# A blocked attention kernel on one core: the scaling of the softmax probabilities moves from Pool to VectorE for three heads of four

## Chip, core and metric

The kernel runs on one core of one Trainium2 chip. The metric is the device time of one execution in microseconds (us), given as the median of several runs. In this text PE is TensorE, ACT is ScalarE, DVE is VectorE, Pool is GpSimd; PEld is TensorE's weight load.

## What is computed

For 8192 tokens of 512 numbers, all in float32, the output is the input plus two branches of its layer norm: a windowed attention and a feed-forward network with ternary weights. The change lies in the attention branch, which is, cut to what matters:

```python
# B = 1, S = 8192, H = 16 heads of Dh = 32, W = 128, nb = S // W = 64 blocks
qkv = (x @ Wqkv + bqkv).reshape(B, S, 3, H, Dh)
...
scores = jnp.einsum('bhnqd,bhnkd->bhnqk', qb, kwin) * scale      # each block sees itself and both neighbours: 128 x 384
mask = (jnp.abs(kpos - qpos) <= W) & (kpos >= 0) & (kpos < S)
scores = jnp.where(mask[None, None], scores, jnp.float32(-1e+30))
attn = jax.nn.softmax(scores, axis=-1)
out = jnp.einsum('bhnqk,bhnkd->bhnqd', attn, vwin)
out = out.reshape(B, H, S, Dh).transpose(0, 2, 1, 3).reshape(B, S, dm)
return out @ Wout + bout
```

## The kernel before

The program has two stages, one after the other. `feed_forward_stage` computes the layer norm, its transpose (written to DRAM in a high and a low part) and the feed-forward branch; it takes the first 1140 us or so. `attention_stage` does the rest and holds the change.

Attention goes over 128 steps t. A step takes one pair of token blocks, i = t // 4, and one group of four heads, c = t % 4. Its two token blocks are the halves b = 0 and b = 1 of the step, so that a step has eight blocks of probabilities of 128 x 384 numbers (128 x 256 at the two ends of the sequence), numbered u = 4 b + h. They lie in one tile, `probs`. For each of them:

- PE computes the scores (L1208), all four heads of a half together, in three passes of high and low parts;
- DVE subtracts the mask and takes the maximum (`find_max`, L1060), from PSUM to `probs`;
- ACT takes the exponential in place and its row sum (`exp`, L989);
- DVE inverts the four sums of a half in one instruction (`invert_sums`, L1067, into `sum_rcp`);
- Pool multiplies each head's probabilities by its inverted sum, in place (`normalise`, L949);
- PE transposes the result, block by block of 128 columns (`turn_probs`, L1222, into `pT_ps`, which has two places);
- ACT copies it to `pT` (`copy_pT`, L999);
- PE multiplies it by the values (`probs_times_values`, L1246), once a step for both halves.

Every engine has one queue, written out by hand and worked off in order. PE's queue for step t is: scores of half 0; then four quarters, each made of the transposes of one head of half 1 of step t-1 (`turn_probs(t - 1, 1, part)`) and six matmuls of a projection of queries and keys for step t+2 (job A, L1139, 128 x 256); scores of half 1; values times probabilities of step t-1; four quarters of transposes of one head of half 0 of step t and three matmuls of a job B (values, L1148, or the output projection, L1157, 128 x 512). Half of the steps have the one kind of job B, half the other. ACT's queue goes head by head: copy of a transposed head, then exponential of another; behind the four heads of half 0 come the copies of new queries and keys (`qk_high`, L1015 and L1018), behind those of half 1 the copy of values (L982, half of the steps). DVE's queue for step t is: the sum of an output block (`add_out`, L1093, half of the steps), `find_max` and `invert_sums` of half 0, the low parts of queries and keys (`qk_low`, L1079 and L1083), `find_max` of half 1, `oT_low` (L1072), `invert_sums` of half 1. Pool's queue has the scaling of both halves, a copy of keys (L955, L956) between them in half of the steps, and an addition of the bias (L960) in the other half.

The semaphores that the change touches: `rcp_done` counts inversions; `normalised` counts scaled heads. `turn_probs` waits for its own head by `normalised` and for a free place of `pT_ps` by `pT_done`.

Of the kernel before, what the change touches and what calls it, by code (L numbers as in the profile page):

```python
# [17 lines left out]
ALU = mybir.AluOpType  # L18
# [8 lines left out]
HC = P // DH  # L27
# [713 lines left out]
def attention_stage(nc, Wqkv, bqkv, Wout, bout, xT_dram, partial, out):  # L741
# [10 lines left out]
    with ctx:  # L752
        def sb(name, shape, dt):
            return ctx.enter_context(nc.sbuf_tensor(name, shape, dt))

        def sem(name):
            return ctx.enter_context(nc.semaphore(name))
# [19 lines left out]
        probs = sb("probs", [P, 2 * HC, 3 * P], F32)  # L777
        neg_max = sb("neg_max", [P, 2 * HC], F32)
        prob_sum = sb("prob_sum", [P, 2 * HC], F32)
        sum_rcp = sb("sum_rcp", [P, 2 * HC], F32)  # L780
# [17 lines left out]
        maxed = sem("maxed")  # L798
        exped = sem("exped")
        rcp_done = sem("rcp_done")  # L800
        normalised = sem("normalised")
        turned = sem("turned")
        pT_done = sem("pT_done")
        pv_done = sem("pv_done")
# [6 lines left out]
        def where(t):  # L811
            return divmod(t, DC)
# [17 lines left out]
        def keys_start(i):  # L830
            return 0 if i % 2 else 2

        def new_keys_at(i):
            return keys_start(i) + 2

        def window(i, b):
            first, last = max(2 * i - 1 + b, 0), min(2 * i + 1 + b, NBLK - 1)
            base = 2 * i - 1 + b
            return slice((first - base) * P, (last - base + 1) * P)
# [5 lines left out]
        def job_a(t):  # L845
            return t + 2 if t + 2 < STEPS else None

        def job_b(t):

            i, c = where(t)  # L850
            if c == 3:
                return ("v", i + 1, 0) if 0 <= i < NT - 1 else None
            if c == 0:
                return ("v", i, 1) if 2 * i + 2 < NBLK else None
            return ("out", i - 1, c - 1) if 1 <= i <= NT else None
# [4 lines left out]
        def pv_bank(t):  # L860
            return (3 * (t + 1) + 1) % 2
# [78 lines left out]

        @block.gpsimd
        def _(pool):
            def normalise(t, b):
                i, _ = where(t)
                cols = window(i, b)
                pool.wait_ge(rcp_done, 2 * t + b + 1)
                for h in range(HC):
                    u = b * HC + h
                    nc.gpsimd.tensor_scalar(probs[:, u, cols], probs[:, u, cols], sum_rcp[:, u:u + 1], None, ALU.mult  # L949
                                            ).then_inc(normalised, 1)  # L950

            def copy_keys(u):
                i, c = where(u)
                pool.wait_ge(qk_done, u + 1)
                nc.gpsimd.tensor_copy(k_hi[:, c, 0:2, :], k_hi[:, c, 4:6, :])  # L955
                nc.gpsimd.tensor_copy(k_lo[:, c, 0:2, :], k_lo[:, c, 4:6, :]).then_inc(keys_copied, 1)  # L956

            def add_bias(i, b):
                pool.wait_ge(out_added, 2 * i + b + 1)
                nc.gpsimd.tensor_tensor(y[:, b, :], y[:, b, :], out_bias[:, :], ALU.add).then_inc(y_done, 1)  # L960

            for u in range(2):
                copy_keys(u)
            for t in range(STEPS + 3):
                b = job_b(t - 1)
                if b and b[0] == "out":
                    add_bias(b[1], b[2])
                if t < STEPS:
                    normalise(t, 0)
                if job_a(t) is not None and where(job_a(t))[0] % 2 == 0:  # L970
                    copy_keys(job_a(t))
                if t < STEPS:
                    normalise(t, 1)
            add_bias(NT - 1, 1)

        @block.scalar
# [73 lines left out]
        @block.vector  # L1050
        def _(dve):
            def find_max(t, b):
                i, _ = where(t)
                cols = window(i, b)
                dve.wait_ge(scored, 2 * t + b + 1)
                if t >= 1:
                    dve.wait_ge(turned, 8 * (t - 1) + HC * (b + 1))
                for h in range(HC):
                    u = b * HC + h
                    nc.vector.tensor_tensor_reduce(out=probs[:, u, cols], in0=score_ps[:, h, cols], in1=mask[:, cols],  # L1060
                                                   scale=-SCORE_SCALE, scalar=3e38, op0=ALU.add, op1=ALU.min,
                                                   accum_out=neg_max[:, u:u + 1]).then_inc(maxed, 1)

            def invert_sums(t, b):
                group = slice(b * HC, (b + 1) * HC)
                dve.wait_ge(exped, 8 * t + HC * (b + 1))
                nc.vector.reciprocal(sum_rcp[:, group], prob_sum[:, group]).then_inc(rcp_done, 1)  # L1067

            def oT_low(t):
                i, c = where(t)  # L1070
                dve.wait_ge(oT_hi_done, t + 1)
                nc.vector.tensor_tensor(oT_lo[:, i % 2, c, :], job_ps[:, pv_bank(t), 0:T],  # L1072
                                        oT_hi[:, i % 2, c, :].bitcast(F32), ALU.subtract).then_inc(oT_done, 1)

            def qk_low(u, bank):
                i, c = where(u)
                half = new_keys_at(i)
                dve.wait_ge(qk_hi_done, u + 1)
                nc.vector.scalar_tensor_tensor(q_lo[:, c, :, :].rearrange("p b t -> p (b t)"), job_ps[:, bank, 0:T],  # L1079
                                               qk_bias[:, c:c + 1],  # L1080
                                               q_hi[:, c, :, :].rearrange("p b t -> p (b t)").bitcast(F32),
                                               ALU.add, ALU.subtract)
                nc.vector.scalar_tensor_tensor(k_lo[:, c, half:half + 2, :].rearrange("p b t -> p (b t)"),  # L1083
                                               job_ps[:, bank, T:2 * T], qk_bias[:, DC + c:DC + c + 1],
                                               k_hi[:, c, half:half + 2, :].rearrange("p b t -> p (b t)").bitcast(F32),
                                               ALU.add, ALU.subtract).then_inc(qk_done, 1)

            def add_out(i, b, number, bank):
                dve.wait_ge(job_filled, number)
                dve.wait_ge(part_here[b], 16 * (i + 1))  # L1090
                if i > 0:
                    dve.wait_ge(y_stored[b], 16 * i)
                nc.vector.tensor_tensor(y[:, b, :], job_ps[:, bank, :], part_in[:, b, :], ALU.add).then_inc(out_added, 1)  # L1093

            dve.wait_ge(k0_hi, 1)
            for c in range(DC):
                last = nc.vector.scalar_tensor_tensor(k_lo[:, c, keys_start(0) + 1, :], job_ps[:, 0, c * P:(c + 1) * P],
                                                      qk_bias[:, DC + c:DC + c + 1],
                                                      k_hi[:, c, keys_start(0) + 1, :].bitcast(F32), ALU.add, ALU.subtract)
            last.then_inc(k0_done, 1)  # L1100
            for u in range(2):
                qk_low(u, u)
            for t in range(STEPS + 3):
                b = job_b(t - 1)
                if b and b[0] == "out":
                    add_out(b[1], b[2], B_NUMBER[t - 1], b_bank(t - 1))
                if t < STEPS:
                    find_max(t, 0)
                    invert_sums(t, 0)
                if job_a(t) is not None:  # L1110
                    qk_low(job_a(t), a_bank(t))
                if t < STEPS:
                    find_max(t, 1)
                if 1 <= t <= STEPS:
                    oT_low(t - 1)
                if t < STEPS:
                    invert_sums(t, 1)
            add_out(NT - 1, 1, B_NUMBER[STEPS + 2], b_bank(STEPS + 2))

        @block.tensor  # L1120
        def _(pe):
# [92 lines left out]
            def turn_probs(t, b, h):  # L1214
                i, _ = where(t)
                u = b * HC + h
                n = 8 * t + u
                if n >= 2:
                    pe.wait_ge(pT_done, n - 1)
                pe.wait_ge(normalised, n + 1)  # L1220
                for w in blocks_seen(i, b):
                    last = nc.tensor.transpose(pT_ps[:, h % 2, w * P:(w + 1) * P], probs[:, u, w * P:(w + 1) * P],  # L1222
                                               ident[:, :])
                last.then_inc(turned, 1)
# [108 lines left out]
```

## Time and profile before

| | |
|---|---|
| median of 3 runs | 2882.3 us (2880.46 to 2883.25) |
| the profiled execution's own time | 2878.27 us |
| its span | 2875.8 us |
| PE busy | 2731.2 us (95%) |
| PEld busy | 2076.6 us (72%) |
| ACT busy | 1667.4 us (58%) |
| Pool busy | 1496.9 us (52%) |
| DVE busy | 1276.2 us (44%) |
| scaling on Pool, L949, 1024 instructions | 1245.6 us busy, 299.8 us idle before them |
| transposes, L1222, 3040 matmuls | 532.6 us busy, 71.3 us idle before them |
| granted TensorE clock, mean of the span | 0.984 of 2.4 GHz |
| the same from 1300 to 2500 us | 1.00 |

The time of an execution is slightly more than its span (here by 2.5 us), which runs from the first to the last instruction in the trace. A matmul's end is modelled and matmuls overlap, so the pace of PE is read from the starts of its instructions, not from its busy share. A line number names the line of the kernel before.

### The profile page before, as it was taken

To read this page: it belongs to the slowest core of one execution; us is meant where nothing else is said; L and a number is where in the kernel's file an instruction comes from. 1 tells how busy PE (TensorE), PEld (TensorE's weight loads), DVE (VectorE), ACT (ScalarE), POOL (GpSimd) and SP (SyncE) were. 2 spreads that over 40 slices of the span, in tenths; PEclk is the share of its full clock that TensorE was granted. 3 is DMA by queue.
4 is the path that set the end of the run, shared out by engine and by line. 5 is a ranking of instruction groups with operands and counts; after the bars stand their busy time and mean duration, and the time that the engine had idled before them with its cause. 6 is when DMAs were issued, how large, how long until landed. Compare 5 with 4: busy or idle time off the path is not lost.

```text
span 2875.8 us, 55762 instructions
## 1 busy us (share of the span) xinstructions
PE 2731.2 (95%) x19728; PEld 2076.6 (72%) x19728; DVE 1276.2 (44%) x3777; ACT 1667.4 (58%) x4261; POOL 1496.9 (52%) x1362
## 2 busy tenths in 40 slices
PE   6999999999999996799999999999999999999997
PEld 4888888888888885567776667676767676767675
DVE  6444444444444442344444444444444444444443
ACT  6333333333333333377777777777777777777775
POOL 0011111111111110278888888888888888888886
PEclk9999999999999998799999999999999999999998
DMA  5222222222222222201111111111111111111010
GB/s 173 65 88 91 78 80 77 76 89 79 73 73 73 78 77 83 66 23 39 38 53 31 38 52 31 55 35 38 53 31 38 53 31 60 31 38 53 31 42 26
DMA packets 189414, 167.93 MB, mean 58 GB/s; under 512 B 11360, under 2 KB 144480, under 8 KB 188688
## 3 DMA queue, kind: packets, MB, share of 16 engines
q1 hardware_dynamic: 189056, 164.93, 18.3%
q8 instruction: 131, 2.15, 0.3%
q14 instruction: 83, 0.68, 0.1%
q0 software_dynamic: 144, 0.17, 0.0%
HBM read 97.95 MB, written 67.11 MB: 57 GB/s over the span
## 4 chain that ended last, share of the span: by engine, by line
PE 20%; ACT 19%; issue 9%; POOL 6%; DVE 5%; DMA 0%; SPq 0%; ACTq 0%; POOLq 0%
ACT probs L989 10%; PE job_ps L1139 9%; PE pT_ps L1222 9%; POOL probs L949 6%; ACT pT L999 5%; DVE probs L1060 2%; DVE k_lo L1083 2%; ACT k_hi L1018 2%; ACT q_hi L1015 2%; ACT oT_hi L1007 1%; DVE sum_rcp L1067 1%; PE job_ps L1258 0%; PE job_ps L1157 0%; PE job_ps L1148 0%; DMA xT_lo<-xT 0%
## 5 line engine op out<-in xcount | busy, mean ns | idle before, releaser
L949 POOL TENSOR_SCALAR probs<-probs,sum_rcp 128x384 f32<-128x384 f32 (+1 forms) x1024 | 1245.6, 1234 | 299.8 <-DVE sum_rcp L1067 299.8
L989 ACT ACTIVATE probs<-probs,neg_max 128x384 f32<-128x384 f32 (+1 forms) x1024 | 633.0, 618 | 179.7 <-DVE neg_max L1060 179.7
L999 ACT COPY pT<-pT_ps 128x384 f32<-128x384 f32 (+1 forms) x1024 | 486.2, 475 | 249.0 <-PE pT_ps L1222 199.2
L1222 PE MATMUL pT_ps<-ident,probs 128*128 128x128 f32 x3040 | 532.6, 284 | 71.3 <-POOL probs L949 67.1
L1222 PEld LDWEIGHTS pT_ps<-ident,probs 128*128 128x128 f32 x3040 | 316.0, 141 | 349.3 <-issue 273.7
L496 ACT ACTIVATE relu<-up_ps,fc_scale 128x512 f32<-128x512 f32 x256 | 176.2, 688 | 655.4 <-PE up_ps L627 655.4
L1060 DVE CUSTOM_DVE_ANT_0 probs<-score_ps,mask 128x384 f32<-128x384 f32 (+1 forms) x1024 | 504.0, 548 | 72.4 <-PE score_ps L1208 69.4
L456 POOL TENSOR_TENSOR f_y<-f_y,part_in 128x512 f32<-128x512 f32 x64 | 87.4, 1396 | 665.1 <-DVE f_y L561 665.1
L570 DVE SCALAR_TENSOR_TENSOR sq<-up_ps,relu 128x512 f32<-128x512 f32 x256 | 176.9, 691 | 530.1 <-ACT relu L496 529.7
L637 PE MATMUL down_ps<-proj_T,sq_hi 128*128 128x512 f32 x1024 | 408.8, 399 | 0.3 <-DVE sq_lo L553 0.2
L639 PE MATMUL down_ps<-proj_T,sq_lo 128*128 128x512 f32 x1024 | 404.3, 395 | 0.0
L623 PE MATMUL up_ps<-f_xT_hi,fc_T 128*128 128x512 f32 x1024 | 399.3, 390 | 1.4 <-DVE low L541 1.4
L625 PE MATMUL up_ps<-f_xT_lo,fc_T 128*128 128x512 f32 x1024 | 399.3, 390 | 0.0
L1067 DVE RECIPROCAL sum_rcp<-prob_sum 128x4 f32<-128x4 f32 x256 | 45.5, 178 | 758.4 <-ACT probs L989 758.4
L1139 PE MATMUL job_ps<-xT_hi,wqkv_hi 128*128 128x256 f32 x1024 | 330.4, 323 | 0.1
L1139 PE MATMUL job_ps<-xT_lo,wqkv_hi 128*128 128x256 f32 x1024 | 287.3, 281 | 0.0
L1139 PE MATMUL job_ps<-xT_hi,wqkv_lo 128*128 128x256 f32 x1024 | 286.1, 279 | 0.0
L637 PEld LDWEIGHTS down_ps<-proj_T,sq_hi 128*128 128x128 f32 x1024 | 193.4, 189 | 42.8 <-DVE sq_lo L553 1.1
L623 PEld LDWEIGHTS up_ps<-f_xT_hi,fc_T 128*128 128x128 f32 x1024 | 192.3, 188 | 44.1 <-DVE low L541 2.2
L639 PEld LDWEIGHTS down_ps<-proj_T,sq_lo 128*128 128x128 f32 x1024 | 193.0, 188 | 43.1
L625 PEld LDWEIGHTS up_ps<-f_xT_lo,fc_T 128*128 128x128 f32 x1024 | 192.3, 188 | 42.5
L989 ACT ACTIVATION_READ_ACCUMULATOR probs<-probs,neg_max 128x1 f32 x1024 | 198.7, 194 | 0.0
(127 smaller groups left out, 4063.0 us busy)
## 6 DMA issues: line engine op xcount, KB each, us to landing
xT_hi<-xT SPq DMA_DIRECT2D x66, 256.0 KB, 3.9
xT_lo<-xT SPq DMA_DIRECT2D x66, 256.0 KB, 4.4
f_x_in<-in_L_attn_x SPq DMA_DIRECT2D x64, 256.0 KB, 3.0
xT<-f_xT_hi SPq DMA_DIRECT2D x64, 256.0 KB, 2.6
xT<-f_xT_lo SPq DMA_DIRECT2D x64, 256.0 KB, 2.8
part_in<-in_L_attn_x SPq DMA_DIRECT2D x64, 256.0 KB, 3.5
partial<-f_y SPq DMA_DIRECT2D x64, 256.0 KB, 2.0
ff_in<-partial SPq DMA_DIRECT2D x64, 256.0 KB, 3.2
```

The source lines that it names most:

```text
L496: nc.scalar.activation(relu[:, s % 2, :], up_ps[:, s % 2, :], ACT.Relu, scale=fc_scale2[:, s:s + 1]).then_inc(relu_done, 1)
L570: nc.vector.scalar_tensor_tensor(sq[:, s % 2, :], up_ps[:, s % 2, :], 0.0, relu[:, s % 2, :], ALU.max, ALU.mult).then_inc(sq_done, 1)
L623: nc.tensor.matmul(up_ps[:, s % 2, :], fc_T[:, k, cols], xT_hi[:, par, k, :], start=(k == 0), stop=False)
L625: nc.tensor.matmul(up_ps[:, s % 2, :], fc_T[:, k, cols], xT_lo[:, par, k, :], start=False, stop=False)
L637: nc.tensor.matmul(down_ps[:, b, :], sq_hi[:, s % 2, t], proj_T[:, s, :], start=(s == 0), stop=False)
L639: last = nc.tensor.matmul(down_ps[:, b, :], sq_lo[:, s % 2, t], proj_T[:, s, :], start=False, stop=(s == FB - 1))
L949: nc.gpsimd.tensor_scalar(probs[:, u, cols], probs[:, u, cols], sum_rcp[:, u:u + 1], None, ALU.mult).then_inc(normalised, 1)
L989: nc.scalar.activation(probs[:, u, cols], probs[:, u, cols], ACT.Exp, bias=neg_max[:, u:u + 1], scale=-1.0, accum_out=prob_sum[:, u:u + 1] ...
L999: nc.scalar.copy(pT[:, h, first + seen.start:first + seen.stop, :].rearrange("p w t -> p (w t)"), pT_ps[:, h % 2, seen.start * P:seen.stop ...
L1060: nc.vector.tensor_tensor_reduce(out=probs[:, u, cols], in0=score_ps[:, h, cols], in1=mask[:, cols], scale=-SCORE_SCALE, scalar=3e38, op0= ...
L1139: last = nc.tensor.matmul(job_ps[:, bank, is_k * T:(is_k + 1) * T], w[:, k, col:col + P], tokens, start=(m == 0), stop=(m == PASSES * DC - 1))
L1222: last = nc.tensor.transpose(pT_ps[:, h % 2, w * P:(w + 1) * P], probs[:, u, w * P:(w + 1) * P], ident[:, :])
```

## The change

DVE now inverts the sums of two heads at a time and scales heads 0 and 1 of a half behind the first inversion and head 2 behind the second. Pool scales head 3 alone, released by the second inversion. PE waits for heads 0 to 2 by `normalised`, which DVE counts up, and for head 3 by `last_head_normalised`, which Pool counts up. DVE waits for its own inversion by `rcp_done` before it scales.

```diff
@@ gpsimd
-            def normalise(t, b):
+            def normalise_last_head(t, b):
                 i, _ = where(t)
                 cols = window(i, b)
-                pool.wait_ge(rcp_done, 2 * t + b + 1)
-                for h in range(HC):
-                    u = b * HC + h
-                    nc.gpsimd.tensor_scalar(probs[:, u, cols], probs[:, u, cols], sum_rcp[:, u:u + 1], None, ALU.mult
-                                            ).then_inc(normalised, 1)
+                u = b * HC + HC - 1
+                pool.wait_ge(rcp_done, 2 * (2 * t + b) + 2)
+                nc.gpsimd.tensor_scalar(probs[:, u, cols], probs[:, u, cols], sum_rcp[:, u:u + 1], None, ALU.mult
+                                        ).then_inc(last_head_normalised, 1)
@@ vector
-            def invert_sums(t, b):
-                group = slice(b * HC, (b + 1) * HC)
-                dve.wait_ge(exped, 8 * t + HC * (b + 1))
-                nc.vector.reciprocal(sum_rcp[:, group], prob_sum[:, group]).then_inc(rcp_done, 1)
+            def normalise(t, b):
+                i, _ = where(t)
+                cols = window(i, b)
+                for pair in range(2):
+                    first = b * HC + 2 * pair
+                    heads = slice(first, first + 2)
+                    dve.wait_ge(exped, 8 * t + first + 2)
+                    nc.vector.reciprocal(sum_rcp[:, heads], prob_sum[:, heads]).then_inc(rcp_done, 1)
+                    dve.wait_ge(rcp_done, 2 * (2 * t + b) + pair + 1)
+                    for u in range(first, first + 2):
+                        if u % HC < HC - 1:
+                            nc.vector.tensor_scalar(probs[:, u, cols], probs[:, u, cols], sum_rcp[:, u:u + 1], None,
+                                                    ALU.mult).then_inc(normalised, 1)
@@ tensor, turn_probs
-                pe.wait_ge(normalised, n + 1)
+                if h == HC - 1:
+                    pe.wait_ge(last_head_normalised, 2 * t + b + 1)
+                else:
+                    pe.wait_ge(normalised, (HC - 1) * (2 * t + b) + h + 1)
```

In DVE's queue the calls of `invert_sums` become calls of `normalise` at the same places. This is the piece of DVE's queue between the maxima of the two halves of a step in the middle of the attention, before:

```order
L1060 ISA probs,neg_max<-score_ps,mask 128x384
L1060 ISA neg_max 128x1
L1067 RECIPROCAL sum_rcp<-prob_sum 128x4 [waits exped]
L1079 SCALAR_TENSOR_TENSOR q_lo<-job_ps,qk_bias,q_hi 128x256 [waits qk_hi_done]
L1083 SCALAR_TENSOR_TENSOR k_lo<-job_ps,qk_bias,k_hi 128x256
L1060 ISA probs,neg_max<-score_ps,mask 128x384 [waits turned,scored]
```

and the same piece with the change:

```order
L1059 ISA probs,neg_max<-score_ps,mask 128x384
L1059 ISA neg_max 128x1
L1070 RECIPROCAL sum_rcp<-prob_sum 128x2 [waits exped]
L1074 TENSOR_SCALAR probs<-probs,sum_rcp 128x384 [waits rcp_done]
L1074 TENSOR_SCALAR probs<-probs,sum_rcp 128x384
L1070 RECIPROCAL sum_rcp<-prob_sum 128x2 [waits exped]
L1074 TENSOR_SCALAR probs<-probs,sum_rcp 128x384 [waits rcp_done]
L1087 SCALAR_TENSOR_TENSOR q_lo<-job_ps,qk_bias,q_hi 128x256 [waits qk_hi_done]
L1091 SCALAR_TENSOR_TENSOR k_lo<-job_ps,qk_bias,k_hi 128x256
L1059 ISA probs,neg_max<-score_ps,mask 128x384 [waits turned,scored]
```

Three multiplications and a second inversion now stand ahead of the low parts of queries and keys; between the maxima of half 1 and those of the next step the same five instructions stand, ahead of `add_out` where there is one.

This is Pool's queue over a bit more than a step, before:

```order
L960 TENSOR_TENSOR y<-y,out_bias 128x512 [waits out_added]
L949 TENSOR_SCALAR probs<-probs,sum_rcp 128x384 [waits rcp_done]
L949 TENSOR_SCALAR probs<-probs,sum_rcp 128x384 x3
L955 COPY k_hi<-k_hi 128x256 [waits qk_done]
L956 COPY k_lo<-k_lo 128x256
L949 TENSOR_SCALAR probs<-probs,sum_rcp 128x384 [waits rcp_done]
L949 TENSOR_SCALAR probs<-probs,sum_rcp 128x384 x3
```

and with the change:

```order
L959 TENSOR_TENSOR y<-y,out_bias 128x512 [waits out_added]
L948 TENSOR_SCALAR probs<-probs,sum_rcp 128x384 [waits rcp_done]
L954 COPY k_hi<-k_hi 128x256 [waits qk_done]
L955 COPY k_lo<-k_lo 128x256
L948 TENSOR_SCALAR probs<-probs,sum_rcp 128x384 [waits rcp_done] x2
```

Each run of four scalings has become one. PE's and ACT's queues keep their order.

## Rows read from the trace of the kernel before

**Rows 1.** Waits from 1500 to 2800 us: total us, times, longest us.
```profile
PE pT_ps L1222 <- POOL probs L949: 42.8, 100, 0.4
```
**Rows 2.** Timeline of Pool, two halves of a step: start us, us, instructions.
```profile
2000.40 4.91 POOL L949 TENSOR_SCALAR probs<-probs,sum_rcp 128x384 f32<-128x384 f32 x4 [1.14 <-DVE sum_rcp L1067]
...
2007.40 4.91 POOL L949 TENSOR_SCALAR probs<-probs,sum_rcp 128x384 f32<-128x384 f32 x4 [0.85 <-DVE sum_rcp L1067]
```
**Rows 3.** Timeline of PE, one step (in brackets idle time before).
```profile
2000.56 0.45 PE L1208 MATMUL score_ps<-k_hi,q_hi 32*128 32x384 f32 x4
...
2001.02 0.34 PE L1208 MATMUL score_ps<-k_lo,q_hi 32*128 32x384 f32 x4
2001.79 0.52 PE L1222 MATMUL pT_ps<-ident,probs 128*128 128x128 f32 x3 [0.43 <-POOL probs L949]
...
2003.02 0.52 PE L1222 MATMUL pT_ps<-ident,probs 128*128 128x128 f32 x3
...
2008.80 0.53 PE L1222 MATMUL pT_ps<-ident,probs 128*128 128x128 f32 x3
...
2013.61 0.45 PE L1208 MATMUL score_ps<-k_hi,q_hi 32*128 32x384 f32 x4
```
**Rows 4.** Timeline of PE in the first steps, with scaled probabilities ready or none needed.
```profile
1194.40 0.28 PE L1208 MATMUL score_ps<-k_lo,q_hi 32*128 32x256 f32 x4
1194.80 0.39 PE L1139 MATMUL job_ps<-xT_hi,wqkv_hi 128*128 128x256 f32 x1
...
1200.52 0.38 PE L1222 MATMUL pT_ps<-ident,probs 128*128 128x128 f32 x2
1200.66 0.48 PE L1148 MATMUL job_ps<-wqkv_hi,xT_hi 128*128 128x512 f32 x1
...
1201.59 0.48 PE L1148 MATMUL job_ps<-wqkv_hi,xT_hi 128*128 128x512 f32 x1
...
1222.08 0.37 PE L1139 MATMUL job_ps<-xT_hi,wqkv_hi 128*128 128x256 f32 x1
...
1222.87 0.49 PE L1222 MATMUL pT_ps<-ident,probs 128*128 128x128 f32 x3
1223.12 0.36 PE L1139 MATMUL job_ps<-xT_hi,wqkv_hi 128*128 128x256 f32 x1
```
**Rows 5.** Timeline of DVE around the inversions of both halves.
```profile
2007.13 0.18 DVE L1067 RECIPROCAL sum_rcp<-prob_sum 128x4 f32<-128x4 f32 x1 [3.72 <-ACT probs L989]
2007.86 0.48 DVE L1079 SCALAR_TENSOR_TENSOR q_lo<-job_ps,qk_bias,q_hi 128x256 fp32r<-128x256 f32 x1 [0.55 <-ACT k_hi L1018]
...
2008.65 0.55 DVE L1060 CUSTOM_DVE_ANT_0 probs<-score_ps,mask 128x384 f32<-128x384 f32 x1
...
2013.17 0.18 DVE L1067 RECIPROCAL sum_rcp<-prob_sum 128x4 f32<-128x4 f32 x1 [2.19 <-ACT probs L989]
2013.71 0.69 DVE L1093 TENSOR_TENSOR y<-job_ps,ff_in 128x512 f32<-128x512 f32 x1 [0.37 <-PE job_ps L1157]
```
**Rows 6.** Timeline of DVE in the weights' preparation: an inversion, then a product that waits for it.
```profile
15.54 0.16 DVE L174 RECIPROCAL inv_scale<-scale 128x1 f32<-128x1 f32 x1
15.73 0.49 DVE L179 TENSOR_SCALAR fc_in<-fc_in,inv_scale 128x512 f32<-128x512 f32 x1
```
**Rows 7.** Feed-forward stage: a DVE line and a Pool line (min/median/max ns), then both timelines at one place.
```profile
L553 DVE TENSOR_TENSOR sq_lo<-sq,sq_hi x256: 679/681/876, 75.2 to 1123.6; 128x512 fp32r<-128x512 f32 x128
...
L456 POOL TENSOR_TENSOR f_y<-f_y,part_in x64: 1258/1296/1796, 141.2 to 1131.5; 128x512 f32<-128x512 f32 x64
...
608.52 0.86 DVE L553 TENSOR_TENSOR sq_lo<-sq,sq_hi 128x512 fp32r<-128x512 f32 x1
...
607.55 2.99 POOL L456 TENSOR_TENSOR f_y<-f_y,part_in 128x512 f32<-128x512 f32 x2
```
**Rows 8.** Timeline of ACT: exponentials of heads 2 and 3 of half 1.
```profile
2011.45 0.63 ACT L989 ACTIVATE probs<-probs,neg_max 128x384 f32<-128x384 f32 x1
...
2012.42 0.63 ACT L989 ACTIVATE probs<-probs,neg_max 128x384 f32<-128x384 f32 x1
```

More of the change, by code:

```diff
@@ L800, in attention_stage @@
         rcp_done = sem("rcp_done")
-        normalised = sem("normalised")
+        normalised, last_head_normalised = sem("normalised"), sem("last_head_normalised")
         turned = sem("turned")
@@ L968, in _ @@
                 if t < STEPS:
-                    normalise(t, 0)
+                    normalise_last_head(t, 0)
                 if job_a(t) is not None and where(job_a(t))[0] % 2 == 0:
@@ L972, in _ @@
                 if t < STEPS:
-                    normalise(t, 1)
+                    normalise_last_head(t, 1)
             add_bias(NT - 1, 1)
@@ L1108, in _ @@
                     find_max(t, 0)
-                    invert_sums(t, 0)
+                    normalise(t, 0)
                 if job_a(t) is not None:
@@ L1116, in _ @@
                 if t < STEPS:
-                    invert_sums(t, 1)
+                    normalise(t, 1)
             add_out(NT - 1, 1, B_NUMBER[STEPS + 2], b_bank(STEPS + 2))
```

## Prediction

> **What bounds the kernel now.** The page's busy shares name PE (95%), but a PE that waits briefly between pipelined matmuls still looks busy, so the starts have to be read. I began with the waits of the attention stage: the transposes wait for the scaling on Pool in every step, 0.43 us each, 100 times in 100 steps [rows 1]. That is the visible part. The rest shows when Pool's timeline is laid beside PE's. Pool scales four heads in 4.91 us, a head every 1.22 us [rows 2], and PE's transposes of one head after the next start at the same distance, 2001.79 and 2003.02, each about 0.15 us behind the end of its head on Pool [rows 2, 3]. So Pool paces PE: a quarter of a step (transposes of a head, then a piece of a job) takes 1.22 us because the next head isn't scaled yet. The view of waits hides this, since the small gaps fall inside the modelled ends of the matmuls.
>
> How fast PE would go by itself shows in the first steps of the attention, where heads lay ready. A quarter with job A goes from 1222.08 to 1223.12, 1.04 us, with three transposes of 0.25 us together. A quarter with job B goes from 1200.66 to 1201.59, 0.93 us, with two transposes of 0.14 us; a third one adds 0.11 us, so 1.04 us too [rows 4]. One step is 13.05 us, 2000.56 to 2013.61 [rows 3].
>
> **The change, part by part.**
>
> *Transposes no longer paced by Pool.* In each half of a step three distances between heads shrink from 1.22 to 1.04 us: 6 x 0.18 = 1.08 us a step. (The fourth quarter ends in scores or in the next part, which waited for nothing.)
>
> *The first transposes behind the scores of half 0.* They start 0.77 us behind the last group of score matmuls [rows 3]. The nearest unhindered case has a job behind scores of 256 columns, 0.40 us [rows 4]; those matmuls last 0.28 us and the ones here 0.34 us, so I take 0.46 us and a gain of 0.31 us. If the wider scores cost in proportion (0.60 us), it is 0.17 us; if nothing, 0.37 us. The head is ready by then: its exponential is two heads earlier than the last one, which released Pool, so about 2 us earlier.
>
> *The first transposes of half 0*, behind values times probabilities, start at 2008.80, 0.15 us behind the end of Pool's first head (2007.40 + 1.24) [rows 2, 3]. The matmuls ahead of them may end just then, so I take 0, with 0.15 us as the other end.
>
> *Three products and one more inversion a half on DVE.* The nearest product waits for its inversion in the same way and takes 0.49 us on 512 columns [rows 6]; in proportion 384 columns would be 0.37 us. I take 0.41 us, with about 0.35 us to the next instruction, and both ends for the range. The first inversion and heads 0 and 1 (about 0.95 us) lie in the 3.72 us, or 2.19 us, in which DVE waits for the last exponential [rows 5]: no cost. The second inversion has the old one's place; head 2 starts 0.2 us behind its start [rows 6] and is out of the way at 0.55 us. In half 0 that still fits before the low parts of the queries, which come 0.73 us behind the inversion since they wait for ACT [rows 5]. In half 1 it meets `add_out`, 0.54 us behind [rows 5]: no delay worth counting. If that cover were gone, each half would lose the product, 0.35 us, on DVE.
>
> *Pool keeps one head a half*, 1.24 us, released 0.27 us behind the inversion's start (2007.13 to 2007.40) [rows 2, 5]. Its transposes are the fourth, 3 x 1.04 us behind the first: hidden by 2 us or more. The copy of keys and the bias addition behind it on Pool come earlier than before.
>
> *Sum.* 1.08 + 0.31 = 1.39 us a step, 11.66 us left. Some 126 of the 128 steps are regular: 175 us. Against the profiled execution's own 2878.3 us that makes 2703 us; the median of the runs is 4.0 us above that execution, so about **2707 us**. With the ends: 1.08 + 0.37 + 0.15 = 1.60 us gives 2681 us; with 0.17 us behind the scores and job B quarters that gain only 0.12 us it is 1.07 us, 2747 us.
>
> *What is late next.* The other loop runs through DVE and ACT, without PE. From the inversion of half 0 to that of half 1 it is 6.04 us [rows 5]: low parts, maxima, exponentials. From there: 0.20 + 0.35 (head 2), 0.74 if there is an `add_out` (0.69 and the step to the next), 0.60 for the first maximum (0.55) until the first exponential, three exponentials at 0.97, 0.75 from the last one to the inversion (2012.42 to 2013.17) [rows 5, 8]: 5.55 us, or 4.81 us without `add_out`. The loop is 11.59 or 10.85 us, 11.22 us on average, below PE's 11.66 us, but not by much.
>
> *The two engines on the same memory.* Head 2 on DVE and head 3 on Pool are released by the same inversion, and both read and write SBUF. In the feed-forward stage a DVE instruction with two SBUF inputs takes 0.68 us, and 0.86 us where Pool adds at the same time; two of Pool's additions there take 2.99 us, where two of the median length would take 2.6 us [rows 7]. So both lose something: 0.18 us the one, 0.4 us the other. In the sum the order decides: DVE's product comes 0.19 us behind the start of the inversion [rows 6], Pool's 0.27 us [rows 2, 5], so DVE is first by 0.08 us and only Pool waits, which has 2 us to spare.
> The Trainium skill (SBUF — State Buffer, "Who interferes with whom") states that a two-port VectorE instruction, and it counts an eligible `tensor_scalar` among them, and a GpSimd instruction exclude each other: the one that starts first holds the shared ports to its end. By that rule, with DVE first, the sum is the same; with Pool first it would be the slower rival below. The trace agrees that the two hinder each other, with 0.18 us on DVE's side; it doesn't show such a product beside Pool.
>
> **The rivals.**
>
> *A, the loop through DVE and ACT takes over.* If the contention holds head 2 back by 0.5 us a half, or the products are longer than taken, the loop grows from 11.22 to about 12.2 us and exceeds PE's 11.66 us. The gain is then 13.05 - 12.2 = 0.85 us a step, 107 us: 2775 us. For it: the loop's margin is only 0.44 us a step, and nearly none with `add_out`. Against it: DVE's lead of 0.08 us, and rows that show small losses.
>
> *B, slower: Pool gets there first.* Then head 2 starts behind all of Pool's head 3, at 0.27 + 1.22 = 1.49 us instead of 0.20 us. In half 0 the low parts of queries and keys, which had 0.18 us of room, start at 1.84 instead of 0.73 us: 1.11 us late, and with them the maxima and exponentials of half 1. In half 1 the maxima of the next step are 1.29 us late. The loop becomes 11.22 + 2.40 = 13.62 us, 0.57 us more than now, 72 us: 2954 us. It turns to slower once the two delays together pass 13.05 - 11.22 + 0.18 = 2.0 us, 1.0 us a half. For it: the lead is only 0.08 us, from two different places of the program, and a start in the trace need not be the moment at which an engine has its ports. Against it: DVE waits for a semaphore of its own, which is the shorter way in both rows.
>
> *C, no change.* PE would be at 1.22 us a quarter for a reason of its own and Pool merely in step with it. Then nothing is gained: 2882 us. Against it stand the quarters of 1.04 us with the same instructions [rows 4].
>
> **How the numbers follow.** My forecast, PE alone sets the pace: 0.78. A: 0.08. B: 0.10. C: 0.04. The predicted time is the forecast's, 2707 us. Its own bounds are 2681 and 2747 us; the range reaches a little below for a product that costs less and up to A's 2775 us and slightly beyond, 2675 to 2785 us, and leaves out B, C and the tails of the others. A measurement here tells 0.2% (6 us) from no change. Faster: forecast and A, 0.86. Same: C, 0.04. Slower: B, 0.10.
>
> **What would show it.** Right: scores of one step to the next about 11.7 us apart; transposes of consecutive heads 1.04 us apart, with next to no wait for DVE or Pool; Pool's scalings 256, a quarter of before, 1.2 us each or up to 0.4 us longer where they lose to DVE; DVE's product of head 2 about 0.2 us behind its inversion and 0.41 us long. Wrong by A: PE waiting for keys or for copies, steps near 12.2 us. Wrong by B: head 2's product 1.3 us or more behind its inversion or three times as long, exponentials late, steps of 13.6 us. Wrong by C: quarters that stay at 1.22 us though the heads are ready.

## Result and the profile after

| | before | after |
|---|---|---|
| median of the runs | 2881.4 us (2878.9 to 2883.3) | 2664.8 us (2662.2 to 2668.4) |
| the profiled execution's own time | 2878.3 us | 2663.5 us |
| its span | 2875.8 us | 2661.7 us |
| step in the steady part (steps 5 to 123) | 13.04 us | 11.43 us |

The ratio of the times is 0.925, with a 95% interval of 0.9234 to 0.9266: the time is 7.5% shorter. The prediction was 2707 us with a range of 2675 to 2785 us. The direction was right and so, in the main, was the mechanism; the gain was 217 us where 175 us were forecast, and the time lies 10 us below the range.

The groups of the page that answer to the table before (line engine op, operands, count | busy us, mean ns | idle us before, and who ended it; DVE's products and paired inversions are new):

```profile
L948 POOL TENSOR_SCALAR probs<-probs,sum_rcp 128x384 f32<-128x384 f32 (+1 forms) x256 | 373.3, 1458 | 959.4 <-DVE sum_rcp L1070 959.4
L1233 PE MATMUL pT_ps<-ident,probs 128*128 128x128 f32 x3040 | 512.6, 277 | 8.2 <-ACT pT L998 7.8
L1074 DVE TENSOR_SCALAR probs<-probs,sum_rcp 128x384 f32<-128x384 f32 (+1 forms) x768 | 298.1, 417 | 18.0
L1070 DVE RECIPROCAL sum_rcp<-prob_sum 128x2 f32<-128x2 f32 x512 | 85.1, 166 | 355.3 <-ACT probs L988 354.7
```

The transposes' idle time has gone from 71.3 to 8.2 us, and what is left of it waits for ACT, not for a scaling. Pool scales a quarter as often but takes 1.46 us for each, not 1.23 us.

PE over a bit more than a step (start us, us). The first four transposes are heads 0 to 3 of half 0; those from 2011.01 on are of half 1, behind the next step's first scores. Rows 3 are the same kinds of instruction before:

```profile
2004.58 0.64 PE L1257 MATMUL job_ps<-pT,values 128*32 128x256 f32 x8
...
2006.02 0.55 PE L1233 MATMUL pT_ps<-ident,probs 128*128 128x128 f32 x3
...
2007.09 0.49 PE L1233 MATMUL pT_ps<-ident,probs 128*128 128x128 f32 x3
...
2008.12 0.49 PE L1233 MATMUL pT_ps<-ident,probs 128*128 128x128 f32 x3
...
2009.15 0.49 PE L1233 MATMUL pT_ps<-ident,probs 128*128 128x128 f32 x3
...
2010.27 0.45 PE L1216 MATMUL score_ps<-k_hi,q_hi 32*128 32x384 f32 x4
...
2010.73 0.35 PE L1216 MATMUL score_ps<-k_lo,q_hi 32*128 32x384 f32 x4
2011.01 0.55 PE L1233 MATMUL pT_ps<-ident,probs 128*128 128x128 f32 x3
...
2012.10 0.49 PE L1233 MATMUL pT_ps<-ident,probs 128*128 128x128 f32 x3
...
2014.17 0.49 PE L1233 MATMUL pT_ps<-ident,probs 128*128 128x128 f32 x3
...
2015.30 0.45 PE L1216 MATMUL score_ps<-k_hi,q_hi 32*128 32x384 f32 x4
...
2021.72 0.45 PE L1216 MATMUL score_ps<-k_hi,q_hi 32*128 32x384 f32 x4
```

Transposes of consecutive heads are 1.03 us apart (2007.09 to 2008.12), where they were 1.22 us [rows 3]; only the first distance of each half is longer, 1.07 and 1.09 us. Behind the scores the transposes come after 0.28 us (2010.73 to 2011.01), where it was 0.77 us. One step, 2010.27 to 2021.72, is 11.45 us.

DVE and Pool at the second inversion of half 0, and, in the last line of DVE, the two products behind the first inversion of half 1:

```profile
2004.44 0.17 DVE L1070 RECIPROCAL sum_rcp<-prob_sum 128x2 f32<-128x2 f32 x1 [1.00 <-ACT probs L988]
2004.64 0.42 DVE L1074 TENSOR_SCALAR probs<-probs,sum_rcp 128x384 f32<-128x384 f32 x1
2005.17 0.48 DVE L1087 SCALAR_TENSOR_TENSOR q_lo<-job_ps,qk_bias,q_hi 128x256 fp32r<-128x256 f32 x1
...
2008.74 0.75 DVE L1074 TENSOR_SCALAR probs<-probs,sum_rcp 128x384 f32<-128x384 f32 x2
```

```profile
2004.71 1.47 POOL L948 TENSOR_SCALAR probs<-probs,sum_rcp 128x384 f32<-128x384 f32 x1 [2.68 <-DVE sum_rcp L1070]
2006.13 0.39 POOL L954 CAST k_hi<-k_hi 128x256 fp32r<-128x256 f32 x1
```

DVE's product starts 0.20 us behind its inversion and 0.07 us ahead of Pool's, takes 0.42 us, and the low parts still come 0.73 us behind the inversion, as in rows 5: the product is over before them. Two products in a row take 0.75 us together.

Where the 214.1 us of span went, from the starts of the scores of every step: 119 steady steps at 1.605 us are 191.0 us; steps 0 to 4 together went from 63.4 to 51.2 us (12.2 us); the last three distances from step to step gained 3.1 us; the piece from the last step's start to the end went from 31.3 to 24.5 us (6.8 us); the stage started 1.0 us earlier.

### The profile page after: what moved, and what is told of

The parts are those of the page before. It is cut to its first block, busy times and chain, and to the rows that moved or that the text cites. A ratio compares the mean times of both kernels' runs of the same rounds, so it can differ in the third digit from the quotient of the medians.

```text
span 2661.7 us, 56018 instructions
## 1 busy us (share of the span) xinstructions
PE 2576.5 (97%) x19728; PEld 2091.7 (79%) x19728; DVE 1602.2 (60%) x4801; ACT 1641.0 (62%) x4261; POOL 625.7 (24%) x594
## 4 chain that ended last, share of the span: by engine, by line
PE 54%; ACT 1%; issue 0%; DVE 0%; DMA 0%; SPq 0%; POOL 0%; POOLq 0%; ACTq 0%
PE pT_ps L1233 14%; PE job_ps L1147 13%; PE job_ps L1156 7%; PE score_ps L1216 7%; PE job_ps L1257 7%; PE job_ps L1165 7%; ACT probs L988 1%; PE job_ps L1269 0%; ACT pT L998 0%; DMA xT_lo<-xT 0%; SPq L914 0%; DVE probs L1059 0%; DVE k_lo L1091 0%; ACT q_hi L1014 0%; ACT k_hi L1017 0%
## 5 line engine op out<-in xcount | busy, mean ns | idle before, releaser
L948 POOL TENSOR_SCALAR probs<-probs,sum_rcp 128x384 f32<-128x384 f32 (+1 forms) x256 | 373.3, 1458 | 959.4 <-DVE sum_rcp L1070 959.4
L1233 PE MATMUL pT_ps<-ident,probs 128*128 128x128 f32 x3040 | 512.6, 277 | 8.2 <-ACT pT L998 7.8
L1233 PEld LDWEIGHTS pT_ps<-ident,probs 128*128 128x128 f32 x3040 | 358.2, 140 | 119.6 <-ACT pT L998 43.0
L1074 DVE TENSOR_SCALAR probs<-probs,sum_rcp 128x384 f32<-128x384 f32 (+1 forms) x768 | 298.1, 417 | 18.0
L1070 DVE RECIPROCAL sum_rcp<-prob_sum 128x2 f32<-128x2 f32 x512 | 85.1, 166 | 355.3 <-ACT probs L988 354.7
```

Source lines behind the costliest of these rows:

```text
L1074: nc.vector.tensor_scalar(probs[:, u, cols], probs[:, u, cols], sum_rcp[:, u:u + 1], None, ALU.mult).then_inc(normalised, 1)
```

## Experiments

Each ratio is to the kernel before on the same chip (2879.5 us for runs 1 to 4, 2879.4 us for runs 5 to 7). In this overview "free" is the time from the start of a half's last inversion to the start of DVE's next instruction that isn't a scaling, in a half that goes on with the queries' low parts. After the change these low parts wait for ACT and not for a product; from run 3 on the products set the time.

| run | scaling of heads 0, 1, 2, 3 | time, us | ratio (95%) | step, us | free, us |
|---|---|---|---|---|---|
| after | DVE, DVE, DVE, Pool; inversions in pairs | 2664.8 | 0.925 (0.9234 to 0.9266) | 11.43 | 0.73 |
| 1 | none | 2662.6 | 0.925 (0.9234 to 0.9265) | 11.43 | |
| 2 | all on Pool; pairs | 2673.4 | 0.928 (0.9267 to 0.9298) | 11.43, one in eight 11.7 | |
| 3 | as after, one inversion | 2944.8 | 1.023 (1.0211 to 1.0245) | 13.60 | 1.88 |
| 4 | all on DVE; pairs | 2695.7 | 0.936 (0.9345 to 0.9376) | 11.65 | 0.86 |
| 5 | as after, Pool let in first | 2712.6 | 0.942 (0.9408 to 0.9439) | 11.81 | 0.97 |
| 6 | as 3, Pool behind DVE | 2787.4 | 0.968 (0.9666 to 0.9698) | 12.33 | 1.21 |
| 7 | all on DVE, one inversion | 2866.4 | 0.995 (0.9937 to 0.997) | 12.94 | 1.54 |

### 1. No scaling at all

```diff
@@ gpsimd, normalise_last_head
-                u = b * HC + HC - 1
-                pool.wait_ge(rcp_done, 2 * (2 * t + b) + 2)
...
+                pass
@@ vector, normalise: the inversions stay
-                    dve.wait_ge(rcp_done, 2 * (2 * t + b) + pair + 1)
-                    for u in range(first, first + 2):
...
@@ tensor, turn_probs
-                if h == HC - 1:
...
+                pe.wait_ge(exped, n + 1)
```

> No engine scales the probabilities; the inversions stay and the transposes wait for the exponentials alone, so the output isn't normalised. Theory 1 (with the change PE's own queue sets the pace, nothing else): steps stay at 11.43 us, the whole at 2655 to 2667 us, since only the last steps can gain. Theory 2 (PE still waits for DVE, Pool or ACT in each step after the change): steps get shorter than 11.35 us and the whole falls below 2650 us.

Measured: 2662.6 us, 2 us (0.1%) from the changed kernel, and the same step of 11.43 us. So what the change leaves of the scaling costs nothing: after it, PE's own pace is the bound. PE behind the scores in this kernel, with no scaling to wait for:

```profile
2009.33 0.34 PE L1208 MATMUL score_ps<-k_lo,q_hi 32*128 32x384 f32 x4
2009.60 0.55 PE L1222 MATMUL pT_ps<-ident,probs 128*128 128x128 f32 x3
```

The transposes stand 0.27 us behind the scores: that is PE's own distance, and the 0.46 us of the prediction was not.

### 2. All four heads on Pool, released in pairs

```diff
@@ gpsimd
-                u = b * HC + HC - 1
-                pool.wait_ge(rcp_done, 2 * (2 * t + b) + 2)
-                nc.gpsimd.tensor_scalar(...).then_inc(last_head_normalised, 1)
+                for h in range(HC):
+                    u = b * HC + h
+                    if h % 2 == 0:
+                        pool.wait_ge(rcp_done, 2 * (2 * t + b) + h // 2 + 1)
+                    nc.gpsimd.tensor_scalar(...).then_inc(normalised, 1)
@@ vector, normalise: the inversions stay, the products go
```

> The sums are inverted two at a time, as in the change, but Pool scales all four heads, the first two behind the first inversion. Theory R (release: the heads came late because Pool began only behind the last exponential of the half; its rate would do, 8 x 1.22 us and about 1 us of other work in 11.43 us): heads 2 and 3 are out 1.5 and 2.7 us behind the second inversion, before PE wants them; steps of 11.43 to 11.6 us, 2665 to 2690 us. Theory P (pace: a head every 1.22 us is too slow for PE's 1.03 us, whoever starts when): six distances a step stay at 1.22 us, steps of 12.5 us, about 2805 us.

Measured: 2673.4 us. No product was moved to DVE, and 206 of the 217 us are there. Pool's timeline:

```profile
2004.14 4.92 POOL L950 TENSOR_SCALAR probs<-probs,sum_rcp 128x384 f32<-128x384 f32 x4
2009.03 1.29 POOL L961 TENSOR_TENSOR y<-y,out_bias 128x512 f32<-128x512 f32 x1
```

Four heads still take 4.92 us, 1.23 us each, slower than PE's 1.03 us a quarter. But Pool starts earlier, two exponentials ahead of the last. Its four heads end at 2005.39 to 2009.06 us, PE's transposes of them start at 2006.11 to 2009.27 us: Pool is 0.7 us ahead at the first head and 0.2 us at the fourth, and PE doesn't catch up within four. What held PE in the kernel before was the rate of Pool together with its late release by the last of four exponentials, and taking away the late release is enough. That taking away the slow rate alone would be enough isn't shown: the runs that do so (3, 6 and 7) bring the late release back by one inversion for four heads, and all of them are slower than this one. Pool is nearly full here: two halves of 4.92 us and 1.29 us for the addition are 11.1 of 11.43 us, and one step in eight slips to 11.7 us.

### 3. Three heads on DVE, but one inversion for all four

```diff
@@ gpsimd
-                pool.wait_ge(rcp_done, 2 * (2 * t + b) + 2)
+                pool.wait_ge(rcp_done, 2 * t + b + 1)
@@ vector
-                for pair in range(2):
...
+                group = slice(b * HC, (b + 1) * HC)
+                dve.wait_ge(exped, 8 * t + HC * (b + 1))
+                nc.vector.reciprocal(sum_rcp[:, group], prob_sum[:, group]).then_inc(rcp_done, 1)
+                dve.wait_ge(rcp_done, 2 * t + b + 1)
+                for u in range(b * HC, b * HC + HC - 1):
+                    nc.vector.tensor_scalar(...).then_inc(normalised, 1)
```

> One inversion of four sums behind the last exponential of the half, as before, then heads 0 to 2 on DVE and head 3 on Pool, as in the change. Theory P (pace is all): DVE delivers a head each 0.35 us, so as fast as the change: 11.43 us, 2665 us. Theory R with the loop through DVE and ACT: all three products now stand between the last exponential and the low parts of queries and keys (in half 0 about 0.5 us late) or the next maxima (in half 1 about 0.7 us late); the loop, 11.22 us by the prediction's sum, becomes 12.4 us and exceeds PE: about 2790 us.

Measured: 2944.8 us, slower than the kernel before, and 155 us off the nearer of the two expectations. Both were wrong. DVE here (each product read by itself), and Pool beside it:

```profile
2010.44 0.18 DVE L1068 RECIPROCAL sum_rcp<-prob_sum 128x4 f32<-128x4 f32 x1 [2.27 <-ACT probs L988]
2010.65 0.42 DVE L1071 TENSOR_SCALAR probs<-probs,sum_rcp 128x384 f32<-128x384 f32 x1
...
2010.99 0.74 DVE L1071 TENSOR_SCALAR probs<-probs,sum_rcp 128x384 f32<-128x384 f32 x1
...
2011.65 0.74 DVE L1071 TENSOR_SCALAR probs<-probs,sum_rcp 128x384 f32<-128x384 f32 x1
2012.32 0.47 DVE L1084 SCALAR_TENSOR_TENSOR q_lo<-job_ps,qk_bias,q_hi 128x256 fp32r<-128x256 f32 x1
```

```profile
2010.71 1.47 POOL L948 TENSOR_SCALAR probs<-probs,sum_rcp 128x384 f32<-128x384 f32 x1 [4.65 <-DVE sum_rcp L1068]
```

The first product takes 0.42 us, the second and third 0.74 us each. DVE is free 1.88 us behind the inversion, and what hangs on it is late: the waits of this kernel from 1500 to 2600 us (total us, times, longest us) show ACT's exponentials waiting for maxima and PE for the low parts of keys:

```profile
ACT probs L988 <- DVE neg_max L1059: 282.8, 162, 2.5
...
PE job_ps L1153 <- DVE k_lo L1088: 50.5, 41, 1.3
PE job_ps L1162 <- DVE k_lo L1088: 49.2, 40, 1.3
```

So the loop through DVE and ACT has taken over from PE. Whether Pool stretched the products or something else did was open; run 6 decides it.

### 4. All four heads on DVE, in pairs

```diff
@@ gpsimd: nothing is scaled
@@ vector, in the loop over a pair
-                        if u % HC < HC - 1:
-                            nc.vector.tensor_scalar(...).then_inc(normalised, 1)
+                        nc.vector.tensor_scalar(...).then_inc(normalised, 1)
```

> Pool scales nothing; DVE scales head 3 behind head 2. The loop through DVE and ACT gets 0.35 us longer in half 1 and 0.17 us in half 0, 11.22 + 0.52 = 11.74 us. If the loop's sum is right, it now exceeds PE's 11.43 us: about 2705 us. If the loop has more room than the sum says (the sum took each piece from the paced kernel), the time stays at 2665 us. If Pool's share had slowed DVE through the shared ports, the products would be shorter than 0.42 us here.

Measured: 2695.7 us, 9 us from the expected value. Two steps in four stay at PE's 11.43 us; the other two, with an `add_out` on DVE, take 11.85 and 11.89 us. So in these two the loop is the next bound. The mean step of 11.65 us mixes both kinds and is not the loop alone. For the steps with `add_out` the expectation's sum is 11.59 + 0.52 = 12.11 us, 0.24 us more than the loop really takes; for the others it is 10.85 + 0.52 = 11.37 us, below PE's 11.43 us, as they show. So the time came within 9 us by a sum that is too long for half of the steps. That is the mechanism of rival A, brought on by one product more a half.

### 5. Pool let in first

```diff
@@ vector, behind the wait for the inversion
+                    if pair == 1:
+                        nc.vector.reciprocal(spare[:, 0:2], prob_sum[:, heads]).then_inc(spare_done, 1)
+                        dve.wait_ge(spare_done, 2 * t + b + 1)
```

> The change, with one more inversion (into a tile that nobody reads) on VectorE between the second inversion and the product of head 2. It takes 0.18 us, so that Pool's head 3 now starts about 0.1 us ahead of that product. The step's loop through VectorE and ACT was 11.65 us in the run in which VectorE was free 0.9 us behind each inversion (0.2 + 2 x 0.35). Theory E, the engine that starts first keeps the other out to its end: the product of head 2 starts when Pool is done, 1.5 us behind the inversion, VectorE is free at about 1.86 us, the step is 11.65 + 2 x 0.96 = 13.57 us, the time about 2938 us, slower than before. Theory S, the two share and VectorE only slows: the product takes 0.74 us, as products 2 and 3 did in the run with one inversion for four heads; VectorE is free at about 1.06 us, the step is about 11.97 us, the time about 2736 us.

Measured: 2712.6 us, steps of 11.51 and 12.1 us, on average 11.81 us. DVE and Pool:

```profile
2008.25 0.17 DVE L1072 RECIPROCAL sum_rcp<-prob_sum 128x2 f32<-128x2 f32 x1 [0.99 <-ACT probs L990]
2008.45 0.17 DVE L1075 RECIPROCAL spare<-prob_sum 128x2 f32<-128x2 f32 x1
2008.65 0.65 DVE L1079 TENSOR_SCALAR probs<-probs,sum_rcp 128x384 f32<-128x384 f32 x1
2009.22 0.47 DVE L1092 SCALAR_TENSOR_TENSOR q_lo<-job_ps,qk_bias,q_hi 128x256 fp32r<-128x256 f32 x1
```

```profile
2008.51 1.24 POOL L950 TENSOR_SCALAR probs<-probs,sum_rcp 128x384 f32<-128x384 f32 x1 [3.98 <-DVE sum_rcp L1072]
```

Pool is 0.14 us ahead and stays at 1.24 us. The product behind it doesn't wait for Pool's end at 2009.75: it is over at 2009.30, 0.65 us long and not 0.42. Theory S held, and theory E missed by 225 us. The time is even 23 us below the 2736 us of theory S, since DVE is free after 0.97 us and not 1.06 us: this product lost 0.23 us to Pool, where those of run 3 lost 0.32 us.

The Trainium skill (SBUF — State Buffer, "Who interferes with whom") says of a DVE instruction in a two-port mode and a GpSimd instruction that whoever issues first holds the shared pair for the whole instruction and the other "fully blocks (not throttle)". Where DVE is second, this trace disagrees, if the product runs in such a mode, which no view tells: it was slowed, not blocked. Where Pool is second, its 1.47 us instead of 1.24 us would roughly fit either reading: held to the end of DVE's product it would lose 0.35 us (2004.71 to 2005.06 in the changed kernel), and it loses 0.23 us.

### 6. As run 3, but Pool waits for DVE's products

```diff
@@ gpsimd, against run 3
-                pool.wait_ge(rcp_done, 2 * t + b + 1)
+                pool.wait_ge(normalised, (HC - 1) * (2 * t + b + 1))
```

> As the run with one inversion for four heads (2944.8 us, step 13.6 us), but Pool's head 3 is released by VectorE's third product and no longer by the inversion, so that Pool never multiplies beside VectorE. No engine has less work. If it was Pool beside them that stretched products 2 and 3 to 0.74 us, the three now take 0.35 us each, VectorE is free 1.25 us behind the inversion and not 1.88, and the step is 11.65 + 2 x 0.35 = 12.35 us: about 2784 us. If the products are that long for a reason of their own (the third one in a row, PE or ACT on the same memory), the time stays at 2945 us or gets longer, since head 3 comes later.

Measured: 2787.4 us, 157 us faster than run 3 with the same instructions, one of which starts later in each half.

```profile
2011.57 0.18 DVE L1068 RECIPROCAL sum_rcp<-prob_sum 128x4 f32<-128x4 f32 x1 [2.26 <-ACT probs L988]
2011.78 1.08 DVE L1071 TENSOR_SCALAR probs<-probs,sum_rcp 128x384 f32<-128x384 f32 x3
2012.78 0.48 DVE L1084 SCALAR_TENSOR_TENSOR q_lo<-job_ps,qk_bias,q_hi 128x256 fp32r<-128x256 f32 x1
```

```profile
2012.96 1.25 POOL L948 TENSOR_SCALAR probs<-probs,sum_rcp 128x384 f32<-128x384 f32 x1 [3.57 <-DVE probs L1071]
```

The three products take 1.08 us, not 1.74 us. It was Pool beside them that stretched them, and that alone cost 1.27 us of the step. The rest of what run 3 lost against the change, 0.9 us a step, goes with the one late inversion: the first two products no longer lie in DVE's wait for the last exponential. The late release also shows at PE, though DVE delivers a head every 0.33 us (waits from 1500 to 2600 us, in 90 steps):

```profile
PE pT_ps L1230 <- DVE probs L1071: 27.7, 90, 0.3
```

The first transposes behind the scores of half 0 come after 0.65 us here and not 0.28 us, so even without the loop these steps would hardly be under 11.8 us (an estimate, 11.43 + 0.37).

### 7. One inversion, all four products on DVE

```diff
@@ gpsimd, against run 3: nothing is scaled
@@ vector, against run 3
-                for u in range(b * HC, b * HC + HC - 1):
+                for u in range(b * HC, (b + 1) * HC):
@@ tensor
+                pe.wait_ge(normalised, n + 1)
```

> One inversion for four heads, all four products on VectorE, none on Pool. VectorE has one product more a half than in the run of 2944.8 us, and Pool beside it is gone. By the loop: VectorE is free 0.2 + 4 x 0.35 = 1.6 us behind the inversion, the step is 11.65 + 2 x 0.7 = 13.05 us, about 2872 us: 70 us faster than with the fourth head on Pool, though VectorE works more. If Pool beside it didn't matter, it is slower than 2945 us.

Measured: 2866.4 us, 78 us faster than run 3 although DVE multiplies a head more and all of them in the way of the loop. Four products take 1.41 us (start us, us):

```profile
2011.92 1.41 DVE L1068 TENSOR_SCALAR probs<-probs,sum_rcp 128x384 f32<-128x384 f32 x4
```

Runs 4, 6, 7 and 3 lie on one line: DVE free after 0.86, 1.21, 1.54 and 1.88 us, steps of 11.65, 12.33, 12.94 and 13.60 us. Each microsecond that DVE is free later in a half lengthens the step by 1.9 us, about one for each half. (In run 4 half of the steps are PE's. The steps with `add_out`, which the loop bounds in all four runs, take 11.87, 12.57, 13.25 and 13.89 us, 2.0 us for each microsecond.) That is the loop the prediction described, with a slope that was argued there and is measured here.

## Why the prediction was right in its mechanism and wrong in its size

**Pool paces PE, and PE alone needs 1.04 us a quarter.** Right in the main: 1.03 us after, 1.07 and 1.09 us for the first distance of a half, and the same without any scaling (run 1). For the six distances the last transposes of each half are needed too. Before, beside rows 3:

```profile
2005.46 0.52 PE L1222 MATMUL pT_ps<-ident,probs 128*128 128x128 f32 x3
...
2006.61 0.45 PE L1208 MATMUL score_ps<-k_hi,q_hi 32*128 32x384 f32 x4
...
2012.46 0.52 PE L1222 MATMUL pT_ps<-ident,probs 128*128 128x128 f32 x3
```

From the first to the fourth head it is 3.67 and 3.66 us before (2001.79 to 2005.46, 2008.80 to 2012.46) and 3.16 and 3.13 us after (2011.01 to 2014.17, 2006.02 to 2009.15). The term of 6 x 0.18 = 1.08 us measured 1.04 us. The fourth quarters, from the last transposes to the next scores, were taken to gain nothing; they shrank from 1.15 us each to 1.13 and 1.12 us, 0.05 us together. One thing was missing in the account: it spoke of Pool's rate alone. Run 2 shows that the late release belonged to it: Pool at the same rate, released earlier, no longer paces PE, and is worth 206 of the 217 us.

**The first transposes behind the scores: this step failed.** It was to gain 0.31 us, with 0.17 and 0.37 us as ends, and gained 0.49 us (0.77 to 0.28 us). The row that was taken as unhindered, the job at 1194.80 in rows 4, was hindered. In the trace of before the weight load of that very job and ACT's copy read:

```profile
1194.16 0.58 ACT L982 COPY values<-job_ps 128x512 f32<-128x512 f32 x1 [1.96 <-PE job_ps L1148]
...
1194.80 0.19 PEld L1139 LDWEIGHTS job_ps<-xT_hi,wqkv_hi 128*128 128x128 f32 x1 [0.32 <-ACT values L982]
```

The job waited 0.32 us for ACT to empty its PSUM bank. The matmul's own row shows no wait, since the wait stood on the weight load. A better bound was at hand in rows 3: from k_hi,q_hi to k_lo,q_hi, two passes of the scores, it is 0.46 us, 0.23 us for one. With that distance behind the third pass the gain is 0.77 - 0.23 = 0.54 us, which would have been the upper end of the term; the measured 0.49 us lies inside it.

**The first transposes behind values times probabilities.** Taken as 0, measured 0.02 us: from the start of that product to the transposes it was 1.46 us and is 1.44 us. Right.

**Sum of a step.** 1.04 + 0.05 + 0.49 + 0.02 = 1.60 us by these places, 1.605 us by the steps, where 1.39 us were forecast. The missing 0.21 us are the 0.18 us of the step that failed, 0.05 us of the fourth quarters and 0.02 us behind values times probabilities, less 0.04 us that the distances fell short. Over 119 steady steps that is 26 us of the 39 us by which the span was missed.

**The ends of the stage were taken as ordinary steps: the second miss.** The prediction counted 126 regular steps. Beyond the 119 steady ones that leaves 7 x 1.39 = 9.7 us for the ends; the nine steps there gained 22.1 us, and the stage started 1.0 us earlier, 23.1 us in all. Part of it may be PE's clock. The windows at the start of the attention, before and then after (window us, its length, busy us of PE, PEld, DVE, ACT and Pool, granted clock, DMA share, GB/s):

```profile
1210.00:1220.00 10.00, 6.71 (x68) 4.81 (x68) 4.88 (x21) 5.91 (x20) 7.91 (x9) 0.76 0.35 105
1220.00:1230.00 10.00, 8.55 (x83) 6.54 (x81) 3.29 (x12) 7.14 (x24) 4.91 (x6) 0.84 0.01 2
1230.00:1240.00 10.00, 8.39 (x79) 7.32 (x75) 2.79 (x13) 5.00 (x17) 6.38 (x6) 0.72 0.01 3
```

```profile
1210.00:1220.00 10.00, 8.23 (x92) 6.55 (x92) 7.32 (x30) 8.20 (x28) 2.61 (x3) 1.00 0.27 79
1220.00:1230.00 10.00, 8.53 (x93) 6.97 (x94) 7.32 (x30) 8.20 (x28) 2.55 (x2) 1.00 0.01 2
1230.00:1240.00 10.00, 10.00 (x101) 7.79 (x99) 7.09 (x27) 8.99 (x28) 2.66 (x2) 1.00 0.00 0
```

Before, PE waited for Pool here (five waits of its transposes, 5.1 us between 1205 and 1245 us), and the granted clock is 0.76, 0.84 and 0.72: a mixture of the levels 2.4 and 1.2 GHz, with 13.6 of the 30 us at the lower one. After, these waits are gone, PE does 92, 93 and 101 matmuls where it did 68, 83 and 79, and the clock stays at 1.00. The same holds for the last piece (0.78 from 2840 us on before, 0.99 from 2637 us on after):

```profile
2840.00:2876.00 36.00, 23.75 (x152) 15.12 (x148) 7.20 (x25) 13.49 (x41) 19.13 (x18) 0.78 0.09 32
```

```profile
2637.20:2662.00 24.80, 14.75 (x125) 9.84 (x124) 9.01 (x31) 9.12 (x30) 7.15 (x6) 0.99 0.13 43
```

The other runs point the same way. In run 7 the clock is 0.66, 0.84 and 0.81 in these three windows and its steps 2 and 3 are 14.3 and 14.7 us, longer than its steady 12.94 us; runs 3 and 6 are alike. In run 2 it is 0.83 in the second window and step 3 is 12.6 us, where it is 10.7 us after the change; run 5 is alike. In runs 1 and 4 it stays at 1.00 and step 3 is 10.6 and 11.0 us. That is an agreement of traces; no run changed the clock alone, and how much of the 13 us is clock and how much is waiting stays open. The page of before has the clock at 8 in its last slice, so a term of its own for the end could have been asked for. For the start the page says little: its slices at 8 and 7 tenths are mostly the passage between the stages (0.57 from 1130 to 1185 us), which is the same after the change.

**Products on DVE.** 0.42 us measured, 0.41 us taken; two in a row 0.75 us; hidden, as run 1 shows to 2 us of the whole.

**Pool's one head.** Taken as hidden by 2 us or more: PE never waited for it longer than 0.4 us, though it grew to 1.47 us. That lay inside the "up to 0.4 us longer" of the prediction.

**Rival A.** It didn't happen, but it was real and near: one product more a half (run 4) brings it, and the loop then costs 0.22 us a step on average. The prediction's sum of the loop was somewhat too long: it gives 11.59 us for a step with `add_out`, and these steps take PE's 11.43 us after the change.

**Rival B.** It would have been wrong even where Pool is first. Its price of 1.49 us for head 2 came from an exclusive hold; run 5 puts Pool first and the product loses 0.23 us, for 2712.6 us and not 2954 us. What it said of the loop, that late products reach the steps through maxima and exponentials, was right, and run 3 shows a kernel that is slower than before in just this way, by stretched products and not by one long block. So its loop was right and its price for head 2 was wrong.

**Rival C** fell with the result: the quarters did shrink, and run 1 has the same ones with no scaling at all.

## What to carry to other kernels

A slow engine that feeds a fast one holds it up by its rate only as far as it starts too late to stay ahead: before moving its work elsewhere, see whether it can start earlier, here by inverting two sums instead of four. When a row is to show an engine's unhindered pace, read the weight load and its releaser too, and give the first and last steps of a stage a term of their own, with the granted clock beside it. Two engines that slow each other belong one behind the other where one of them is in a loop that sets the pace: releasing Pool a microsecond later gained 157 us in run 6.

## What the runs showed of the hardware

- A DVE product of 128 x 384 float32 in SBUF takes 0.42 us alone, 0.33 to 0.34 us to the next one. Beside a Pool product it takes 0.65 us (run 5, Pool 0.14 us ahead) or 0.74 us (run 3, second and third product). It isn't held until Pool ends.
- Pool's product of the same size takes 1.24 us alone or where it is first, and 1.47 us where DVE was 0.06 or 0.07 us ahead. In run 3 it is 1.47 us too, though three DVE products run beside it: it lost 0.23 us to the first and nothing to the others, which lost 0.32 us each. So the one that comes second pays, and by less than the other's length.
- Between 1210 and 1240 us, where PE's transposes waited for Pool before the change, the granted clock was 0.72 to 0.84; after the change, without these waits, it stayed at 1.00. Five of the seven runs show the lower clock there too, at 0.66 to 0.84; no run changed the clock alone.
